# Mixture-of-experts and linear attention in one kernel: when an expert's rows are measured, rooted and normalised

## What is computed

```
x = x + 0.5 * _L0_ffn_ref(_layernorm(x), w_switch, b_switch, w1, b1, w2, b2)
x = x + _L0_attn_ref(_layernorm(x), ...)
x = x + 0.5 * _L0_ffn_ref(_layernorm(x), w_switch, b_switch, w1, b1, w2, b2)

# in _L0_ffn_ref: E = 8 experts, capacity = 0.5 * 4096 / 8 = 256 rows each
routes = softmax(x @ w_switch + b_switch).argmax(-1)
buf_e  = the first 256 rows of each expert                   # (8, 256, 256)
h = relu(einsum('ecd,edh->ech', buf_e, w1) + b1)             # 1024 hidden
y = einsum('ech,ehd->ecd', h, w2) + b2
out = where(keep, y_flat[slot], x)
```

## Time and profile before

| what | value |
|---|---|
| median of 3 runs | 703.06 us (702.52 to 704.05) |
| the profiled execution, its own time | 700.69 us |
| its span | 699.0 us |
| PE busy | 655.5 us, 94% |
| DVE busy | 503.0 us, 72% |
| ACT busy | 448.0 us, 64% |
| POOL busy | 369.8 us, 53% |
| mean granted TensorE clock | 0.975 |

### The profile page before, as it was taken

The page is one execution under the profiler, slowest core; times in us unless marked ns, Lnnn a source line. Parts: engine busy times, 40 slices in busy tenths (PEclk is TensorE's granted clock), DMA queues, the critical chain, the costliest instruction groups (busy, mean ns, idle before and its releaser), DMA issues.

```text
span 699.0 us, 17818 instructions
## 1 busy us (share of the span) xinstructions
PE 655.5 (94%) x6346; PEld 574.9 (82%) x6346; DVE 503.0 (72%) x1350; ACT 448.0 (64%) x895; POOL 369.8 (53%) x535
## 2 busy tenths in 40 slices
PE   7789999998789999999999999999999995899997
PEld 5569999975578898888888888888987772799997
DVE  7874756424578777868878778878766567799992
ACT  5676655513367787767767667776753663788882
POOL 5153664125456545465583764846545563357642
PEclk9879999999999999999999999999999995999999
DMA  7399897414766555544555455564442523567840
GB/s 263 112 296 315 276 304 256 144 46 111 108 105 105 95 78 91 103 85 72 109 82 121 83 89 129 70 113 89 87 82 40 180 92 92 172 218 219 246 161 30
DMA packets 284802, 95.60 MB, mean 137 GB/s; under 512 B 213988, under 2 KB 281664, under 8 KB 284714
## 3 DMA queue, kind: packets, MB, share of 16 engines
q1 hardware_dynamic: 267610, 82.27, 48.7%
q0 software_dynamic: 4992, 11.47, 5.9%
q10 hardware_dynamic: 12112, 0.72, 1.1%
HBM read 65.09 MB, written 29.40 MB: 135 GB/s over the span
## 4 chain that ended last, share of the span: by engine, by line
PE 55%; DVE 7%; issue 4%; POOL 4%; ACT 3%; SPq 2%; DMA 1%; ACTq 1%; POOLq 0%; DVEq 0%
PE bank L1932 49%; PE bank L1941 6%; POOL hids L901 2%; SPq L440 1%; DMA qkv_rows<-feats 1%; DVE den L1765 1%; DVE hn_ L1810 1%; DVE att_ L1763 1%; DMA keys<-qkv_rows 1%; DVE ots L1756 1%; DVE kv_ L1790 1%; POOL sth L886 0%; ACT feats L1125 0%; ACT L1201 0%; POOL stz L870 0%
## 5 line engine op out<-in xcount | busy, mean ns | idle before, releaser
L1932 PE MATMUL bank<-down_w,hids 128*128 128x256 f32 x768 | 104.5, 284 | 1.8 <-POOL hids L901 1.7
L1932 PE MATMUL bank<-hnts,up_w 128*128 128x512 f32 (+1 forms) x432 | 106.0, 382 | 0.1
L901 POOL TENSOR_TENSOR hids<-hid,hids 128x512 fp32r<-128x512 f32 (+1 forms) x68 | 83.3, 1226 | 36.0 <-ACT hids L1177 35.8
L1932 PEld LDWEIGHTS bank<-down_w,hids 128*128 128x128 f32 x768 | 96.6, 188 | 4.8 <-POOL hids L901 3.1
L1932 PE MATMUL bank<-qkv_w,xnts 128*128 128x256 f32 (+1 forms) x384 | 78.3, 352 | 1.5 <-DVE xnts L1776 0.9
L1932 PEld LDWEIGHTS bank<-hnts,up_w 128*128 128x128 f32 x432 | 71.2, 189 | 10.3 <-ACT hids L1177 0.3
L1932 PEld LDWEIGHTS bank<-qkv_w,xnts 128*128 128x128 f32 x384 | 61.7, 192 | 18.9 <-issue 5.8
L867 POOL TENSOR_SCALAR stz<-stz 128x1 f32<-128x1 f32 x32 | 7.2, 226 | 121.6 <-DVE stz L1794 121.6
L1172 ACT ACTIVATE hid<-bank,cols 128x512 f32<-128x512 f32 (+1 forms) x72 | 45.7, 640 | 39.4 <-PE bank L1932 38.0
L1932 PE MATMUL bank<-a_w,xa_h 128*128 128x256 f32 x256 | 60.2, 379 | 0.0
L1932 PE MATMUL bank<-xa_xt,a_w 128*128 128x256 f32 x384 | 55.1, 294 | 0.9 <-DVE xa_xt L1460 0.9
(11 more groups left out here) (292 smaller groups left out, 1562.1 us busy)
## 6 DMA issues: line engine op xcount, KB each, us to landing
qkv_rows<-feats SPq DMA_DIRECT2D x32, 384.0 KB, 3.1
a_raw<-in_L_ffn_w_dram SPq DMA_DIRECT2D x32, 256.0 KB
a_w<-in_L_ffn_w_dram SPq DMA_DIRECT2D x32, 256.0 KB
b_raw<-in_L_ffn_w_dram SPq DMA_DIRECT2D x32, 256.0 KB
b_w<-in_L_ffn_w_dram SPq DMA_DIRECT2D x32, 256.0 KB
mid_rows<-x_all SPq DMA_DIRECT2D x8, 512.0 KB
values<-qkv_rows SPq DMA_DIRECT2D x32, 128.0 KB
late_rows<-x_ SPq DMA_DIRECT2D x8, 512.0 KB, 3.1
```

The lines of the kernel that those rows point to most:

```text
L901: pool.tensor_tensor(hids[1][u % 3][:, 0:w], hid[u % 2][:, 0:w], f32(hids[0][u % 3][:, 0:w]), ALU.subtract).then_inc(s_hidl, 1)
L1932: return pe.matmul(dst, left, right, start=start, stop=stop, skip_group_check=True)
```

## The change

Four things move, and nothing is added or taken away.

DVE measures expert x + 2 in the third unit of expert x (for the first expert of a phase, in its fourth unit), behind that unit's low weights. Before, it measured expert x + 1 at the start of the first unit of x.

POOL makes the root of expert x + 3 between the scatters of expert x and the gathers of x + 4. Before, it made the root of x + 1 as the first thing of expert x's first unit.

DVE normalises expert x + 1 ahead of the low weights of its first unit, and no longer behind them. In the very first unit of phase b, `low_hidden` of that unit also stands ahead of the low weights.

The memsets of `clear_grids` all stand behind the scatters of expert 5, the first expert with no gathers to follow.

```diff
--- before.py
+++ after.py
@@ -810,14 +810,16 @@
                     load_rows(x, ex)
                 for u in range(ex.first * PAIRS, ex.end * PAIRS + 2):
                     x, j = divmod(u, PAIRS)
-                    if j == 0 and ex.first < x < ex.end - 1:
-                        root_rows(x + 1, ex)
-                        if x + 1 == xb.end - 2:
-                            pool.drain()
+                    if x == ex.first and j == PAIRS - 1:
+                        root_rows(x + 2, ex)
+                    if j == 0 and x == xb.end - 3:
+                        pool.drain()
                     if u >= ex.first * PAIRS + 2:
                         px, pj = divmod(u - 2, PAIRS)
                         if pj == PAIRS - 1:
                             send_rows(px, ex)
+                            if px + 3 < ex.end:
+                                root_rows(px + 3, ex)
                             if px + ROWS_AHEAD < ex.end:
                                 load_rows(px + ROWS_AHEAD, ex)
                             if between:
@@ -849,12 +851,13 @@
 
 
             def clear_grids(x):
-                if 1 <= x < 3:
-                    pool.memset(keys[x - 1][:], 0.0).then_inc(s_zeros, 1)
-                    pool.memset(queries[x - 1][:], 0.0).then_inc(s_zeros, 1)
-                    pool.memset(values[x - 1][:], 0.0).then_inc(s_values, 1)
-                    pool.wait_ge(s_values, x)
-                    pool.memset(values[x - 1][:, :, HD], 1.0).then_inc(s_zeros, 1)
+                if x == E - 3:
+                    for i in range(2):
+                        pool.memset(keys[i][:], 0.0).then_inc(s_zeros, 1)
+                        pool.memset(queries[i][:], 0.0).then_inc(s_zeros, 1)
+                        pool.memset(values[i][:], 0.0).then_inc(s_values, 1)
+                        pool.wait_ge(s_values, i + 1)
+                        pool.memset(values[i][:, :, HD], 1.0).then_inc(s_zeros, 1)
 
             run_experts(xa, clear_grids)
             pool.drain()
@@ -1541,10 +1544,10 @@
                 first_rows(ex, meanwhile)
                 for u in range(ex.first * PAIRS, ex.end * PAIRS + 2):
                     x, j = divmod(u, PAIRS)
-                    if u > ex.first * PAIRS and (u - 1) // PAIRS < ex.end and (u - 1) % PAIRS < split_of((u - 1) // PAIRS):
+                    if u > ex.first * PAIRS + 1 and (u - 1) // PAIRS < ex.end and (u - 1) % PAIRS < split_of((u - 1) // PAIRS):
                         low_hidden(u - 1, ex)
                     if x < ex.end:
-                        if j == 0 and x + 1 < ex.end:
+                        if u == ex.first * PAIRS:
                             measure_rows(x + 1, ex)
                         if j == 2 and x + 1 < ex.end:
                             low_rows(x + 1, ex)
@@ -1555,9 +1558,13 @@
                         if pj == PAIRS - 1:
                             finish(px, ex)
                     if x + 1 < ex.end:
-                        low_weights(x + 1, ex, j)
                         if j == 0:
                             norm_rows(x + 1, ex)
+                        if u == ex.first * PAIRS and split_of(x):
+                            low_hidden(u, ex)
+                        low_weights(x + 1, ex, j)
+                    if x + 2 < ex.end and j == (PAIRS - 1 if x == ex.first else 2):
+                        measure_rows(x + 2, ex)
                     if x < ex.end and between:
                         between(u)
```

## The result

The changed kernel ran in 703.53 us (median of 20 runs, 701.95 to 706.83) and the kernel before, on the same chip, in 702.41 (20 runs, 700.07 to 704.05). The ratio is 1.0022, with a 95% interval of 1.0011 to 1.0032: it is slower, by about 1.5 us by the ratio and by 1.1 us by the two medians. The forecast was a small gain. The time fell inside the range given, the sign did not.

What follows compares the result with a forecast made beforehand. PE was taken as the bound, busy 655.5 of 699.0 us. Phase b's 0.1 plus phase a's 0.3 gave a 0.4 us gain, median 703.06 to 702.7, with a range from 700.9 to 703.9.

Steps and rivals of the forecast that it cites:

- The start of phase b: Phase b's first units: DVE normalises earlier, so unit 0's down products lead by 1.84 us, shrinking to 0.13 at unit 4.
- a term of 0.1: Phase b's share of the forecast gain: 0.1 us, with ends of a loss of 0.2 and a gain of 1.84.
- 0.3 was the term: Phase a: root and measuring come earlier and the unit no longer waits, gaining 0.3 of 0.35 us.
- the gap: POOL's free 10.56 us before the scatter at 142.23, into which the memsets, 8.4 us, were to move at no cost.
- The step that failed: Phase b from expert 2 on: root made before it is wanted, DVE's 0.63 us idling gone, PE sets the pace.
- a loss of 0.2: Lower end for phase b, if unit 4's root takes its full 1.73 us and PE goes 0.18 later.
- a unit waiting for its root from expert 3 on: Listed sign that the forecast is wrong: DVE's unit operation still waiting for POOL's root from expert 3 on.
- The rival: Slower: phase b roots late behind two scatters, PE loses up to 0.8 in each of 6 experts, 4.6 us, 707.7; 7%.

Runs made afterwards that it cites:

- e1: Changed kernel with the last expert's root in phase b moved ahead of the two scatters; 702.1 us, ratio 1.0012.
- e2: Changed kernel without POOL's drain in the expert loop of phase b; 706.22 us, ratio 1.0065.
- e6: Changed kernel with POOL's drain moved behind the two scatters and the last expert's root; 701.88 us, ratio 0.9995.
- e5: Changed kernel with the normalising, and low_hidden of unit 0, put back behind the low weights; 702.74 us, ratio 1.0003.
- e8: Changed kernel, last root ahead of the scatters, expert 2 measured at its old place and in phase b normalised behind its weights; 701.1 us, ratio 0.9977.
- e11: Same edits as e8 on the changed kernel, plus the drain moved behind the last root and the two scatters; 701.62 us, ratio 0.9988.
- e4: Kernel before, with only each phase's first unit normalised (in phase b also low_hidden of unit 0) ahead of the low weights; 703.96 us, ratio 1.0027.
- e9: Changed kernel measured once more, with no further edit; 703.67 us, ratio 1.0021.

## Why the prediction was wrong

**The start of phase b was right, step by step.** The leads are those of the table, before less after. Predicted leads 1.84, 1.16, 0.39, 0.13 and 0.02 at units 0, 1, 3, 4 and 6; measured 1.76, 1.14, 0.42, 0.15 and 0.09, and 0.02 at unit 7. The unit before expert 2 waited 0.94 us for its root (0.9 was forecast). The root's first operation took 0.57 at 611.24 and the second 0.73, where I had let them last 0.62 and 0.73. The measured sum of the phase's start is 0, for a term of 0.1.

**Phase a and the memsets.** In the pair of traces phase a is 0.50 us shorter (0.3 was the term), and the five rounds from expert 2's down products (65.06) to expert 7's (129.76) take 64.70 us, 12.94 each, where the earlier trace rows have 129.58 - 64.53 = 65.05. Over all traces the two orders lie 0.4 us apart in their medians, with a spread of 1 us within one order, so the term has the right size as far as can be told, and is not shown to a tenth. The eight memsets lie between 131.84 and 140.21, in the gap, and delay no scatter, as forecast.

**The step that failed** is "From expert 2 on the root is made before it is wanted, DVE's 0.63 of idling is gone, and PE sets the pace as before", and with it the term of 0.1 us for phase b, whose lower end, "a loss of 0.2", priced only the start: the phase lost 1.93. The sentence holds for experts 3 to 6 (DVE names no wait for their roots, and at experts 4 to 6 POOL waits for the measuring instead, for expert 6 at 655.79 after 2.56 us idle). For expert 7 the root was wanted 3.31 us before it was made, which the prediction itself had named as a sign of being wrong ("a unit waiting for its root from expert 3 on"). I had drawn the rest of the phase from one steady expert and had not read POOL's timeline near its end, where `pool.drain()` stands for 7 us. The diff has that line, and neither the walk nor the sum does.

**The rival was the right mechanism with the wrong place and count.** "The root of expert x + 3 stands behind two scatters on POOL. If it came later than its unit, DVE would stand with the two weight operations (1.2 us) uncovered" is what the rows of unit 24 show. I priced it at 0.8 in each of 6 experts. It cost 1.93 in one, since the uncovered 1.20 met a root that was itself later, by the drain. What spoke against it, the measuring two units earlier, was no answer: POOL's queue, not the measuring, came last. e1, e2 and e6 each take one part away (the scatters ahead of the root, the drain, the drain's place), and in each the 1.93 is gone whole; e5 gives the cover back, and with it 0.82 of the root's lateness, and is left with 0.09 of slack. So it took the drain and the scatters ahead of the root together, and DVE's order, unit before weights, for the size.

**The sum as it came out:** start of phase b 0, the last expert's root 1.93, and phase b entered 0.36 earlier: about +1.5 us. That 0.36 is not phase a's term alone: phase a began 0.63 later (its first down product at 52.11, 51.48 before), took 0.50 less, and the stretch from its end to phase b took 0.49 less, and all three vary by as much from run to run. That the time still fell inside the range is luck: the range reached up there for the spread of the three runs and not for this loss.

What stays open is where the time of the middle stage goes from run to run: in these profiled runs the stretch between the first attention products and the first up product there took 28.8 to 32.0 us, whatever the kernel. Whether the gain of e8 and e11 is real beyond the 0.33 us of the trace was not settled either.

## What to carry to other kernels

A steady round of a loop doesn't show the last ones: where a change orders an engine's queue anew, read that engine's timeline in the first, a middle and the last iterations, and look for what stands there once (a drain, a barrier, a special case). Two operations that a wait covers are a reserve: putting the waiting operation ahead of them is free only while its input is always early, so ask which input can be late, and when. And a lead is worth nothing by itself: e4 gained half a microsecond at the start, and behind it the loop of scatters, gathers and root ran 0.48 us slower in every round.

## What the runs showed of the hardware

- **A drain on POOL amid indirect transfers took 6.1 to 7.6 us of its queue** (6.83 before, 7.49 after, 6.96 in e6, 7.56 in e9, and 6.13 in e1, up to the root that follows it there), and leaving it out added 4.7 us between the last scatter and the end of the span.
- **POOL's small root operations last by what DVE does beside them.** `xb_rstd<-xb_mv`, two elements a partition, takes 0.23 to 0.25 us while DVE stands, 0.56 to 0.57 beside operations of 0.66 us on two SBUF inputs, and 0.75 to 0.77 beside one of 0.69 that starts with it (the rows at 672.96, 668.47 and 671.33). It ends just behind the DVE operation: at 669.03 where low_hidden ended at 668.95 (e6), at 672.10 where the weight operation ended at 672.01 (before). The Trainium skill, SBUF — State Buffer, section Who interferes with whom, has a DVE instruction with two SBUF inputs contending with a GpSimd instruction that reads SBUF; these rows agree.
- **The issue of an indirect transfer took 0.94 to 2.4 us of POOL, with the same tiles** (one, behind the drain of e4, 3.09; most below 1.3 or above 2.0). Every one above 2 us in phase b lay beside at least 1.8 us of DVE operations, and those beside an idle DVE took 0.97 to 1.00, but some of 0.95 to 1.17 lay beside a busy DVE throughout (that at 604.38 before). So every slow one had DVE busy beside it, and a busy DVE does not suffice; what decides was not tried. The length repeats from expert to expert and from run to run with the order of the instructions (the second gather of a round 0.97 before, 1.11 in e4 and e5, 2.03 after), so it can be read once in a trace and reckoned with.
